# Ternary weights by way of int16: rounding in place, one clip pass, and new opening lists in a fused mLSTM and BitNet feed-forward kernel

## What is computed

```python
def _weight_quant(w):
    scale = 1.0 / jnp.clip(jnp.mean(jnp.abs(w)), 1e-05)
    return jnp.clip(jnp.round(w * scale), -1.0, 1.0) / scale
def _act_quant(x):
    scale = 127.0 / jnp.clip(jnp.max(jnp.abs(x), -1, keepdims=True), 1e-05)
    return jnp.clip(jnp.round(x * scale), -128.0, 127.0) / scale
def _bitlinear(x, w):
    return jnp.einsum('bsi,oi->bso', _act_quant(x), _weight_quant(w))
...
x = x + _L0_xattn_ref(_layernorm(x), ctx_1024, ctx_1024, ...)
x = x + _L0_ffn_ref(_layernorm(x), w_gate, w_up, w_down)
```

## Time and profile before

| | us |
|---|---|
| median of 3 runs (lowest, highest) | 654.17 (652.73, 654.47) |
| the profiled execution | 655.61 |
| its span from first to last instruction | 653.8 |

### The profile page before, as it was taken

The page is one execution under the profiler, slowest core; times in us unless marked ns, Lnnn a source line. Parts: engine busy times, 40 slices in busy tenths (PEclk is TensorE's granted clock), DMA queues, the critical chain, the costliest instruction groups (busy, mean ns, idle before and its releaser), DMA issues. The chain is left out here.

```text
span 653.8 us, 13097 instructions
## 1 busy us (share of the span) xinstructions
PE 588.2 (90%) x3768; PEld 387.9 (59%) x3828; DVE 539.2 (82%) x1427; ACT 467.8 (72%) x713; POOL 319.1 (49%) x487
## 2 busy tenths in 40 slices
PE   8777677798989999999999999999989997899995
PEld 7677554575646656666656655665656653465442
DVE  3376687879899898989899889989898899968762
ACT  3836977877668786779677875878677967856652
POOL 3168873455463466455556366356645455334100
PEclk9988799899999999999999999999999999999998
DMA  8697401410252122510262025212250041000001
GB/s 329 269 314 263 149 2 65 161 53 14 82 177 82 49 80 92 168 48 2 80 209 87 9 81 176 80 48 81 73 183 32 15 147 64 18 17 17 17 21 45
DMA packets 34210, 63.78 MB, mean 98 GB/s; under 512 B 2688, under 2 KB 19200, under 8 KB 31616
## 3 DMA queue, kind: packets, MB, share of 16 engines
q1 hardware_dynamic: 33600, 62.92, 27.9%
q10 hardware_dynamic: 576, 0.44, 0.3%
HBM read 54.84 MB, written 8.52 MB: 97 GB/s over the span
## 5 line engine op out<-in xcount | busy, mean ns | idle before, releaser
L647 PE MATMUL GU<-WQ,xqT 128*128 128x512 bf16 x975 | 237.8, 387 | 13.0 <-DVE FF L1457 7.1
L647 PEld LDWEIGHTS GU<-WQ,xqT 128*128 128x128 bf16 x1024 | 97.9, 99 | 114.9 <-issue 13.8
L678 PE MATMUL ACC<-WQ,FF 128*128 128x512 bf16 x501 | 116.7, 384 | 3.6 <-ACT FF L1006 1.7
L985 ACT ACTIVATE FF<-GU,cgu 128x512 f32<-128x512 f32 x128 | 86.3, 687 | 20.2 <-PE GU L647 19.3
L1457 DVE TENSOR_TENSOR FF<-FF,GU 128x512 f32<-128x512 f32 x128 | 85.3, 680 | 16.7 <-ACT FF L985 10.7
L678 PEld LDWEIGHTS ACC<-WQ,FF 128*128 128x128 bf16 x512 | 49.8, 99 | 61.0 <-ACT FF L1006 3.7
L993 ACT ACTIVATE FF<-FF,magic,hs 128x1024 f32<-128x1024 f32 x64 | 78.9, 1237 | 2.9 <-DVE hs L1488 2.9
L953 ACT ACTIVATE work<-AT,pb 128x128 f32<-128x128 f32 x128 | 47.8, 452 | 23.3 <-POOL pb L1840 22.9
L594 PE MATMUL AT<-vext,CT 128*128 128x129 f32 x256 | 50.3, 287 | 3.4 <-ACT gate_parts L891 2.1
L1862 POOL TENSOR_TENSOR work<-work,norm_bc 128x512 f32<-128x512 f32 x32 | 42.8, 1336 | 20.8 <-ACT work L953 20.8
L1826 POOL TENSOR_SCALAR pb<-den 128x4 f32<-128x4 f32 x32 | 8.1, 252 | 90.7 <-DVE den L1393 90.6
(11 more groups left out here) (126 smaller groups left out, 1211.1 us busy)
## 6 DMA issues: line engine op xcount, KB each, us to landing
bc<-gate_rows SPq DMA_DIRECT2D x32, 512.0 KB, 6.3
xin<-in_x SPq DMA_DIRECT2D x32, 256.0 KB, 3.0
kT<-in_ctx_t SPq DMA_DIRECT2D x8, 1024.0 KB, 4.9
vext<-in_ctx SPq DMA_DIRECT2D x32, 256.0 KB, 3.6
out<-FF SPq DMA_DIRECT2D x32, 256.0 KB, 2.4
WQ<-in_w_gate SPq DMA_DIRECT2D x4, 1024.0 KB, 13.1
FF<-in_w_up SPq DMA_DIRECT2D x4, 1024.0 KB, 14.6
WQ<-in_w_down SPq DMA_DIRECT2D x2, 1024.0 KB, 6.8
```

The lines of the kernel that those rows point to most:

```text
L647: last = nc.tensor.matmul(dst, xqT[:, b, P * k:P * (k + 1)], w[:, k, 512 * j:512 * (j + 1)], start=(k == 0), stop=(k == KC - 1))
L678: last = nc.tensor.matmul(ACC[:, :], hT[:, b % 2, P * k:P * (k + 1)], WD[:, 4 * place(2, k // 4) + k % 4, :], start=(k == 0), stop=(k == J ...
L985: nc.scalar.activation(sg[:, j % 2, :], GU[:, 2 * (j % 2), :], ACT.Silu, scale=cgu[:, b, 0:1]).then_inc(silu_done, 1)
```

## The change

The magic constant goes for weights. A quarter now takes two passes: `weight_round` multiplies by the factor and writes int16 into the final place (`whole`, a view of `ternary` as int16), and `weight_clip` reads the int16, takes the maximum with -1 and the minimum with 1 in one instruction, and writes bf16 in place. DVE rounds quarters (0,1) and (0,0); ACT rounds (1,3), (1,2), (2,1) and (2,0); POOL rounds the other six; DVE clips all twelve. Semaphores `w_whole` replace `w_lifted`, and waits for space that was read (loads, `copy_hT`, the first `multiply` of block 1, `weight_sum` of m = 2) are for the rounding and no longer for the finished weights. The column with the negative constant is dropped, so that the tile `magic` has one column. `keep_floor` waits for DVE's own semaphore `bstat`, in the loop too. The rest of the loop is as before; the lists of all five openings are new.

```diff
@@ functions
-        magic = sb("magic", [P, 2])
+        magic = sb("magic", [P, 1])
+        def whole(m, c):
+            return ternary(m, c).bitcast(I16)
             def load_quarter(m, c):
                 if m == 2:
-                    sp.wait_ge(w_done[(2, 3, 7, 5)[c]], 1)
+                    sp.wait_ge(w_whole[(2, 3, 7, 5)[c]], 1)
@@ scalar
-            def weight_sign(m, c):
-                act.wait_ge(w_lifted[4 * m + c], 1)
+            def weight_round(m, c):
+                act.wait_ge(w_scaled, m + 1)
                 if m == 1:
-                    act.wait_ge(w_done[c // 2], 1)
+                    act.wait_ge(w_whole[c // 2], 1)
                 if m == 2 and c > 1:
-                    act.wait_ge(w_done[6 + c], 1)
-                nc.scalar.activation(ternary(m, c), staged(m, c), ACT.Sign,
-                                     bias=magic[:, 1:2]).then_inc(w_done[4 * m + c], 1)
+                    act.wait_ge(w_whole[6 + c], 1)
+                nc.scalar.activation(whole(m, c), staged(m, c), ACT.Identity,
+                                     scale=w_factor[:, m:m + 1]).then_inc(w_whole[4 * m + c], 1)
@@ vector
             def keep_floor(g):
+                bstat_at, = values(dve, g * 4)
+                if live(bstat_at):
+                    dve.wait_ge(bstat, bstat_at)
                 V.tensor_copy(floor_n[:, :], cols[:, 2, :]).then_inc(dve_seq, 1)
-            def weight_lift(m, c):
-                V.tensor_scalar(staged(m, c), staged(m, c), w_factor[:, m:m + 1], MAGIC, ALU.mult, ALU.add).then_inc(w_lifted[4 * m + c], 1)
+            def weight_round(m, c):
...
+                V.tensor_scalar(whole(m, c), staged(m, c), w_factor[:, m:m + 1], None, ALU.mult).then_inc(w_whole[4 * m + c], 1)
             def weight_clip(m, c):
-                dve.wait_ge(w_lifted[4 * m + c], 1)
...
-                V.tensor_scalar(ternary(m, c), staged(m, c), MAGIC, -1.0, ALU.subtract, ALU.max).then_inc(dve_seq, 1)
...
-                V.tensor_scalar(ternary(m, c), ternary(m, c), 1.0, None, ALU.min).then_inc(w_done[4 * m + c], 1)
+                dve.wait_ge(w_whole[4 * m + c], 1)
+                V.tensor_scalar(ternary(m, c), whole(m, c), -1.0, 1.0, ALU.max, ALU.min).then_inc(w_done[4 * m + c], 1)
@@ gpsimd
-                G.tensor_scalar(staged(m, c), staged(m, c), w_factor[:, m:m + 1], MAGIC, ALU.mult, ALU.add).then_inc(w_lifted[4 * m + c], 1)
+                G.tensor_scalar(whole(m, c), staged(m, c), w_factor[:, m:m + 1], 1.0, ALU.mult, ALU.mult).then_inc(w_whole[4 * m + c], 1)
```

The new lists, as far as the prediction needs them (the old ones are in the kernel above). Dots leave out the rest; in gpsimd's list `weigh_q` of chunk 0, which only waits for `bc`, and `fade` of chunk 0, which does nothing, are left out too:

```diff
@@ sync, from the start
+ x(0,0) x(0,1) k(0) x(0,2) x(0,3) x(1,0) quarter(0,0) x(1,1) quarter(0,1) v(0,0) v(0,1) x(1,2)
+ quarter(0,2) x(1,3) quarter(0,3) x(2,0) quarter(1,1) spread(0,0) spread(0,1) spread(0,2)
+ quarter(1,0) quarter(1,2) quarter(1,3) k(1) spread(0,3) v(0,2) quarter(2,1) v(0,3) quarter(2,0)
+ quarter(2,2) x(2,1) quarter(2,3) x(2,2) v(1,0) k(2) spread(1,0) x(2,3) spread(1,1) v(1,1) ...
@@ tensor
+ warm 13, transpose_xn(0,0), warm 10, transpose_xn(0,1), score(0,0), warm 1, score(0,1),
+ transpose_xn(0,2), warm 1, score(0,2), transpose_xn(0,3), warm 1, score(0,3), warm 3,
+ transpose_gates(0), warm 22, transpose_rows(0), warm 4, weight_total(0), warm 26, numerators(0,0),
+ warm 19, state_step(0,0), transpose_xn(1,0), numerators(0,1), weight_total(1), warm 25,
+ state_step(0,1), warm 2, numerators(0,2), warm 9, transpose_xq(0,0), warm 4, weight_total(2),
+ warm 2, state_step(0,2), gate_up(0,0,0), transpose_xq(0,1), numerators(0,3), gate_up(0,0,1),
+ transpose_xn(1,1), gate_up(0,0,2), gate_up(0,0,3), score(1,0), transpose_xn(1,2), score(1,1),
+ transpose_xq(0,2), score(1,2), transpose_xn(1,3), gate_up(0,1,0), score(1,3), gate_up(0,1,1),
+ transpose_gates(1), gate_up(0,1,2), transpose_xq(0,3), gate_up(0,1,3), state_step(0,3),
+ transpose_rows(1), gate_up(0,2,0), transpose_xn(2,0), gate_up(0,2,1), transpose_h(0,0,0),
+ transpose_xn(2,1), transpose_h(0,0,1), score(2,0), score(2,1), gate_up(0,2,2), numerators(1,0), ...
@@ scalar
+ ... copy_scores(0,3), exp_soft(0), log_soft(0), sum(0,2), exp_rows(0), sum(0,3), exp_decay(0,0),
+ abs_sums(0,0), sum(1,0), exp_decay(0,1), sum(1,1), norm_heads(0,0), sum(1,2), exp_decay(0,2),
+ sum(1,3), abs_sums(0,1), round(1,3), round(1,2), norm_heads(0,1), sum(2,0), copy_qT(1,0),
+ exp_decay(0,3), sum(2,1), abs_sums(0,2), sum(2,2), round_x(0,0), sum(2,3), norm_heads(0,2),
+ round_x(0,1), copy_xqT(0,0), silu(0,0,0), copy_xqT(0,1), abs_sums(0,3), silu(0,0,1), round(2,1),
+ silu(0,0,2), norm_heads(0,3), silu(0,0,3), copy_qT(1,1), copy_scores(1,0), round_x(0,2),
+ copy_qT(1,2), copy_scores(1,1), copy_xqT(0,2), round(2,0), copy_qT(1,3), copy_scores(1,2),
+ silu(0,1,0), round_x(0,3), copy_scores(1,3), silu(0,1,1), exp_soft(1), log_soft(1), exp_rows(1), ...
@@ vector
+ ... sum_gates(0), forget_rows(0), x_stats(1,1), cumulate_rows(0), weight_scale(0), round(0,1),
+ x_stats(1,2), copy_cols(0), keep_decay(0,0), decay_argument(0,0), keep_decay(0,1), round(0,0),
+ weigh(0,0), keep_decay(0,2), clip(0,3), keep_floor(0), decay_argument(0,1), head_stats(0,0),
+ x_norm(1,1), decay_argument(0,2), weigh(0,1), clip(0,0), state_update(0,0), x1_stats(0,0),
+ weight_scale(1), x1_scale(0,0), head_stats(0,1), keep_decay(0,3), decay_argument(0,3), clip(0,1),
+ weigh(0,2), x_stats(1,3), state_update(0,1), x1_stats(0,1), x1_scale(0,1), head_stats(0,2),
+ clip(1,1), clip(1,0), clip(0,2), weigh(0,3), clip(1,2), clip(1,3), state_update(0,2), x_stats(2,0),
+ weight_scale(2), multiply(0,0,0), head_stats(0,3), x_norm(1,2), multiply(0,0,1), clip(2,1), ...
+ sum_gates(1), forget_rows(1), clip(2,0), multiply(0,1,0), multiply(0,1,1), cumulate_rows(1),
+ clip(2,2), h_scale(0,0), multiply(0,1,2), h_max(0,1), x_norm(2,1), multiply(0,1,3), clip(2,3),
+ copy_cols(1), h_scale(0,1), keep_decay(1,0), decay_argument(1,0), copy_hT(0,0), state_update(0,3), ...
@@ gpsimd
+ ... round(0,3), x_rstd(1,1), x_rstd(1,2), weigh_keys(0,0), head_scale(0,0),
+ residual(0,0), weigh_keys(0,1), round(0,2), x1_rstd(0,0), round(1,1), head_scale(0,1),
+ residual(0,1), weigh_keys(0,2), x1_rstd(0,1), round(1,0), head_scale(0,2), ... round(2,3),
+ round(2,2), ...
```

More of the change, by code:

```diff
@@ L1133, in opening @@
+                weight_round(1, 2)
+                norm_heads(0, 1)
+                weight_sum(2, 0)
+                copy_qT(1, 0)
+                exp_decay(0, 3)
+                weight_sum(2, 1)
+                abs_sums(0, 2)
+                weight_sum(2, 2)
+                round_x(0, 0)
+                weight_sum(2, 3)
+                norm_heads(0, 2)
+                round_x(0, 1)
                 copy_xqT(0, 0)
-                exp_decay(0, 3)
                 silu(0, 0, 0)
-                norm_heads(0, 2)
@@ L1660, in opening @@
-                keep_decay(0, 2)
-                x_norm(1, 0, 1)
-                weigh(0, 1)
-                weight_clip(0, 1)
-                state_update(0, 0)
-                weight_scale(1)
-                weight_lift(0, 0)
-                x1_stats(0, 0, 0)
-                head_stats(0, 1)
-                x1_scale(0, 0, 0)
-                x_stats(1, 3, 1)
-                weight_clip(0, 0)
-                decay_argument(0, 2)
-                weigh(0, 2)
-                state_update(0, 1)
@@ L1675, in opening @@
-                keep_decay(0, 3)
-                x_stats(2, 0, 2)
-                head_stats(0, 2)
-                decay_argument(0, 3)
-                x1_stats(0, 1, 0)
-                x_norm(1, 1, 1)
-                x1_scale(0, 1, 0)
+                x_norm(1, 1, 1)
+                decay_argument(0, 2)
+                weigh(0, 1)
+                weight_clip(0, 0)
+                state_update(0, 0)
+                x1_stats(0, 0, 0)
+                weight_scale(1)
+                x1_scale(0, 0, 0)
@@ new lines, in opening @@
+                head_stats(0, 1)
+                keep_decay(0, 3)
+                decay_argument(0, 3)
+                weight_clip(0, 1)
+                weigh(0, 2)
+                x_stats(1, 3, 1)
+                state_update(0, 1)
+                x1_stats(0, 1, 0)
+                x1_scale(0, 1, 0)
+                head_stats(0, 2)
+                weight_clip(1, 1)
+                weight_clip(1, 0)
+                weight_clip(0, 2)
+                weigh(0, 3)
+                weight_clip(1, 2)
@@ L1689, in opening @@
[L1689 to L1701 removed]
+                x1_stats(0, 2, 0)
+                x1_scale(0, 2, 0)
```

388 lines of the change are left out of this document (190 added, 198 removed), and 2 rows, old and new, of the table OPENING_AT.

## The result

| | before | after |
|---|---|---|
| median, us (20 runs each, beside each other) | 655.18 (648.83 to 658.85) | 661.76 (655.49 to 666.64) |
| ratio, 95% interval | 1 | **1.0089 [1.0059, 1.0119]** |
| profiled execution, its span | 655.61, 653.8 | 666.64, 664.8 |

The change makes the kernel 0.9% slower. The forecast was 650.0 (643 to 657.5), faster. The profiled execution of after is 4.9 us above the median of its kernel, and was the longest of the 20, so some of its lateness is that of this one execution and not of the list. How much can be told from run e13 in the table: up to the transposed gates of chunk 1 its list is the same as after's, and its gates of chunk 1 are summed at 105.18, where this execution has 110.63.

The account below looks back on a forecast made before the run. The loop was taken as bound by PE with DVE close behind and unchanged, so only its earlier start counted. The terms summed to -4.5 us, 655.6 to 651.1, less 1.4 to the median: 650 us, range 643 to 657.5.

Parts of the forecast that it names:

- The passes: Opening's weight passes: clip 0.69 us, rounding 1.28 on DVE, 2.0 on ACT, 1.97 on POOL.
- Rival 3: The clip is a slow pass, 1.21 us for 0.69 or more; gain shrinks to -1.5, 652.7 us; chance 0.08.
- First numerators: Chunk 0's first numerators start at 41.0 us, +0.6; the high end of this term is +2.7.
- The links: Block chain through AT: numerators 1 at 51.4, numerators 2 at 66.7, norm 2 ending at 76.5 us.
- The lock between POOL and DVE: Shared ports: total time of such DVE passes matters, not their number; 10.2 to 10.9 us, so the sum stays.
- First gate_up: First feed-forward gate product, in the opening, starts at 78.0 us, +2.2.
- rival 1: Slower, late weights: nine sums and late first factor stay on the path; 656.4 to 658.5 us; chance 0.17.
- Gates and rows of chunk 1: Gates at 101.2 us, -4.2; rows at 108.8, gate_up(0,1,3) and the last state_step filling part of PE's wait.
- The wait for score(2,0): End of chunk 1: score(2,0) waits for its bank behind state_update(0,3) at 119.9 us; numerators(1,0) at 127.5.
- The clock: Chunk 1 to its numerators: 5.9 us gained at full clock, 2.4 at PE's lower level, 4.5 taken.
- rival 2: Given back: chunk 1's gates 4 us early, late state_update(0,3) and slow clock eat it; 653 to 654 us; chance 0.16.
- The spread: Whole kernel: range 643 to 657.5 us; three runs of before differ by 0.3%, about 2 us.

Follow-up runs that it names:

- e13: Changed kernel with only 24 products of ones added in PE's gaps of chunk 1: 655.65 us, ratio 0.9991 to the kernel before.
- e14: Changed kernel with transpose_rows(1) ahead of gate_up(0,1,3), copy_xqT(0,3) ahead of exp_rows(1), and all added products of ones: 653.45 us, ratio 0.9951.
- e12: Changed kernel with 51 products of ones added ahead of state steps 0 to 2 and 24 in chunk 1, a repeat: 653.64 us, ratio 0.9958.
- e3: Changed kernel with four clips earlier, copy_xqT(0,0) ahead of norm_heads(0,2), two gate_up ahead of state_step(0,2), two products of ones dropped: 662.54 us, ratio 1.009.
- e15: e14 with state_update(0,3) right behind cumulate_rows(1) on DVE: 655.25 us, ratio 0.9952 to the kernel before.
- e2: Changed kernel with the first scores and transposes of chunk 0 on PE and ACT in the order of before: 659.23 us, ratio 1.0043.
- e10: Changed kernel with only the 51 products of ones ahead of state steps 0 to 2, none in chunk 1: 658.88 us, ratio 1.0029.

## Why the prediction was wrong

**The passes.** Right, each within 0.02 us; that int16 is as cheap as bf16 for the clip was an assumption and held. Rival 3 is out.

**First numerators.** 41.0, with 2.7 us to the high end, was named; 43.27 came, in an execution that was already 1.8 us late at 18.7 us by lower clock (0.7 ahead of 14.3 us, the rest at 15.5) and then had its 52 products of ones in 7.67 us. e13 has no such delay and comes at 42.88: there the 52 took 8.89 us, as in before's row of 8.87, the high end of this term, where I had chosen the low.

**The links.** Blocks 0 and 1 were to give 4.5 us up to numerators(0,2) (71.24 to 66.7) and gave 0.7 in after and 2.4 in e13. Block 2 failed outright. I put the end of norm 2 at 76.5 from ACT's and DVE's counts; in the profile after `norm_heads(0,2)` begins at 80.36, and with it the first `gate_up` comes at 84.29 for 78.0. `head_scale` of 4.0 us for 2.6 beside five clips is 1.4 of that. Most of the rest was there before block 2's norm: `numerators(0,2)` came 3.9 us later than forecast.

**The lock between POOL and DVE.** The prediction looked at the rule of the Trainium skill, "SBUF — State Buffer", section Who interferes with whom, and let the sum stay, because the total time of the passes hardly changed. e14 has the plainest rows; DVE first, then POOL:

```profile
72.56 1.89 DVE L1557 TENSOR_SCALAR WQ<-WQ 128x2048 bf16<-128x2048 int16 x3
74.36 0.69 DVE L1389 TENSOR_TENSOR CT<-CT,scores 128x512 f32<-128x512 f32 x1
74.97 1.29 DVE L1557 TENSOR_SCALAR WQ<-WQ 128x2048 bf16<-128x2048 int16 x2
...
72.83 3.47 POOL L1844 TENSOR_SCALAR pb<-den 128x4 f32<-128x4 f32 x1 [1.58 <-DVE den L1407]
76.39 0.19 POOL L1846 TENSOR_SCALAR pb<-mv_b 128x4 f32<-128x4 f32 x1
```

An instruction that before has at 0.19 us with no such pass beside it (85.90) ends at 76.30, with the last of DVE's five clips and the `weigh` among them (76.26). By that rule such a DVE pass holds the shared ports for its whole length; the trace agrees, and shows more, that POOL may get no turn between passes that follow each other. It need not be so: beside the same passes the first instruction took 0.46 or 0.47 us in after, e12 and e13, as in this row of e13,

```profile
74.95 0.47 POOL L1844 TENSOR_SCALAR pb<-den 128x4 f32<-128x4 f32 x1 [1.58 <-DVE den L1407]
```

and the whole `head_scale` 4.0 us, for 5.6 in e14. With one clip and the `weigh` beside it (e3) it took 3.2. So how many such passes stand in one piece ahead of a small POOL instruction that the chain waits for counts beside their total. The new list put five there. In the time of the kernel this is a small part: e3, with four of them moved away, is no faster.

**First gate_up, and rival 1.** Rival 1 had the right sign with the wrong cause. It decides, the prediction said, if score(1,0) is no earlier than 90.1, and it came at 94.66 (92.53 in e13). But e3 brings the first `gate_up` to 77.20 and stays at 1.009, and e13 is at 0.9991 with its first `gate_up` at 82.48: late weights aren't what costs.

**Gates and rows of chunk 1.** The 4.2 us at the gates never came: e13, without the delays of after's execution, sums them at 105.18, where before has 105.43. I expected `gate_up(0,1,3)` and the last state step to fill PE's wait for the rows. In after, `gate_up(0,1,2)` itself waits 2.33 us for DVE's `multiply`, and the rows wait for `TPB`: I had not looked at which transposes stand ahead of the rows in `TPB`, and at ACT's copy for them, moved behind two table loads. Of 16.7 us that numerators(1,0) are late against the forecast (144.18 less 127.5), 9.4 are there at the gates of chunk 1, 2.7 more come up to the rows, and 4.6 behind them. In e13 the same three are 4.0, 2.6 and -1.1: what after's one execution adds is at the gates, what the clock of chunk 1 adds is behind the rows.

**The wait for score(2,0).** The prediction had it wait for the late `state_update(0,3)`. e15 shows that it doesn't: the wait is that of `transpose_xn(2,1)` for `copy_hT(0,0)`, ahead of it in PE's list. Its terms don't add up either: 119.9 and 2.1, 0.7, 2 and 1.7 give 126.4 and not 127.5.

**The clock: the step that failed.** The prediction had for the end of chunk 1 "4.2 + 1.7 = 5.9 us gained at full clock", "2.4 gained" at the lower level, and "I take 4.5". It took the level as a property of the stretch that the old trace shows, the same for the new list, and priced it only for two scores and a product, at 3.5 us, where e10 against e13 has 4.6; rival 2 named it too and let it eat the gain, no more. The runs show that the level answers to the list: over 125 to 150 us it went from 0.86 to 0.73 in after, e2 and e10 alike, and holding it in chunk 1 alone takes the ratio from 1.0089 to 0.9991 [0.9957, 1.0025], which is all of the loss within the interval. What remains then is no loss and no gain from the lists: with the clock held for the most part the loop starts at 195.0 to 196.0 with the new lists and 194.3 to 195.3 with the old. So there were two errors: the gain of 4.5 us isn't there even at full clock, as the gates of chunk 1 come no earlier than before (105.18 for 105.43), the rows come 2.9 us later (115.42 for 112.57), and where e14 wins the rows back DVE's and ACT's chain through the feed-forward takes it up; and the clock makes a loss of what should have been a draw. The spread was taken too small as well: from three runs of before within 0.3%, where twenty span 10.0 us, 1.5%.

**What stays open.** Why the new lists' gaps bring the clock down for longer than the old ones'. In both it falls near 126 us; before is back at full level at 133.4, e10 at 139. That PE had 16.58 of 25 us busy in e10's window ahead of it and 18.80 in before's is a difference that fits, and the lists say where it comes from. Before has score(2,0) ahead of `transpose_xn(2,1)`, the new list behind it and `transpose_h(0,0,1)`. So in before this score runs in PE's wait, at full level, and only score(2,1) runs at the lower one:

```profile
122.33 0.95 PE L537 MATMUL AT<-gate_q,qT 128*128 128x8 f32 x8
...
124.78 0.63 PE L517 MATMUL TPB<-ident,xn 128*128 128x128 f32 x4 [0.70 <-DVE FF L1501]
...
127.55 1.71 PE L537 MATMUL AT<-gate_q,qT 128*128 128x8 f32 x8
```

The kernel after with score(2,0) back in its old place wasn't tried, so this is argued and not shown. It would also need `state_update(0,3)` early, as in e15. Open too is what the early gate products are worth with their clips in time and the clock held.
